# Two edge tiles ahead of the next two, and W_ih's loads later: the opening of a graph network kernel

## The chip, the cores and the metric

The kernel runs on one core of a Trainium2 chip. The metric is the device time of one execution in microseconds (us), lower is better. TensorE is called PE, VectorE DVE, ScalarE ACT, GpSimd POOL; SyncE (SP) issues most of the DMAs.

## The reference, cut to what matters

```python
h = layernorm(x)                                   # x: 10000 nodes x 512
m_in = concatenate([h[src], edge_attr], axis=1)    # 2500 edges x (512 + 128)
m = relu(m_in @ W1.T + b1) @ W2.T + b2             # edge network
agg = segment_sum(m, dst, num_segments=10000)      # sums over edges of one node
gi = agg @ W_ih.T + b_ih                           # 3 x 512 gate inputs
gh = h @ W_hh.T + b_hh
r = sigmoid(i_r + h_r); z = sigmoid(i_z + h_z); n = tanh(i_n + r * h_n)
h_new = (1 - z) * n + z * h
x = x + h + batchnorm(h_new)
x = x + mixture_of_experts(layernorm(x))           # 8 experts, the best 2, one shared
```

All arrays are float32. Matrix products are done in three passes over a high and a low part of each operand (high x high, high x low, low x high), so each operand has to be split: ACT copies out the high part, DVE subtracts it for the low part.

## The kernel before, in words

The 2500 edges are padded to 2560, 20 tiles of 128 rows, in five groups of four tiles (SUP = 4). For each group: POOL gathers the source rows of x by indirect DMA (gather_source, L697), DVE takes their statistics (stats), POOL makes the scale and shift (front), ACT normalises the rows (normalise, L806), PE transposes them four blocks a tile (transposes, L1271), ACT takes the high part of the transposed rows (transposed_hi, L817) and DVE the low part (transposed_lo, L954). The fifth block of each edge tile is the edge attributes, which arrive already transposed by DMA (attributes, L589) and are split by attributes_hi (ACT, L801) and attributes_lo (DVE, L929). layer1 (PE, L1290) then multiplies with W1, 15 matmuls of 512 columns a tile. It alternates between banks 0 and 1. DVE adds b1 (messages, L980), which empties the bank, ACT and DVE split the result (messages_hi L824, messages_lo L985), and sums (L1338) adds up rows of equal destination by a matmul with a 0/1 matrix (compare, L967) into banks 0, 1, 6 and 7. These sums are split by sums_hi (L829) and sums_lo (L998).

Once, between the second group's first layer and its sums, fused_weights multiplies W2 with W_ih (L1306 and L1321), so that the second layer and the gate product become one product. For it the four chunks of W_ih (768 KB each) are loaded, split on ACT (wih_hi_of, L801) and on DVE (wih_lo_of, L929), and W2 likewise (w2_lo, L1105). All later groups do layer1, product and sums. After the edges a loop runs over 79 tiles of nodes.

Every engine has its own queue, whose order is written out by hand; engines wait for one another on semaphores, and an instruction that waits holds all that follow on its engine. SP's queue holds the loads in the order of the program text, and a wait in it holds the loads behind it.

The waits that the prediction uses: layer1 of group 1 waits for attributes_lo(1) and, before tiles 0 and 1, for a_lo_done (the sums in banks 0 and 1 have been read); before tiles 2 and 3 it waits for msg_done (messages of tiles 0 and 1 have emptied the bank):

```python
if j < 2:
    wait_from(pe, a_lo_done, DK * (g - 1) + j + 1)
else:
    pe.wait_ge(msg_done, SUP * g + j - 1)
```

SP's attributes(1) waits for the end of layer1(0) (l1), since it overwrites the first group's attributes. A gather for tile j of group 1 waits until the same tile of group 0 is transposed (t_e). keep_running(n) issues n transposes of the identity on PE into a bank that nobody reads.

Of the kernel before, what the change touches and what calls it, by code (L numbers as in the profile page):

```python
# [34 lines left out]
def gnn_ffn(nc, x, src, dst, dst_rows, dst_back, attr_t, w1t, b1, w2, b2, wih_t, whh_t, whh, x_cols, b_ih, b_hh, gamma, beta,  # L35
# [5 lines left out]
    DK = D // P  # L41
# [7 lines left out]
    SUP = 4  # L49
# [103 lines left out]
    w2_hi = place("w2_hi", [P, DK, D], F32R)  # L153
# [429 lines left out]
    with nc.Block() as block:  # L583
        @block.sync
        def _(sp):
# [25 lines left out]
            sp.dma_start(w2_raw[:, :, :], w2v).then_inc(w2_in, 16)  # L611
            sp.dma_start(row_i[:, :], dst_rows[0:1, :].broadcast_to((R, SW))).then_inc(row_in, 16)
            sp.dma_start(b2_col[:, :], b2).then_inc(b2_in, 16)
            for k in range(2):
                sp.dma_start(wih_raw[:, k, :], wihv[:, k, :]).then_inc(wih_in[k], 16)
            sp.dma_start(ig_bias[:, :], bcast(b_ih)).then_inc(bias_in, 16)
            sp.dma_start(ig_bhh[:, :], bcast(b_hh[0:2 * D])).then_inc(bias_in, 16)
            for k in range(2, DK):
                sp.dma_start(wih_raw[:, k, :], wihv[:, k, :]).then_inc(wih_in[k], 16)
            sp.dma_start(all_dst_i[:, :], dst_back.broadcast_to((R, E))).then_inc(all_dst_in, 16)  # L620
            attributes(1)
            for n, of in enumerate((gamma, beta, run_mean, run_var)):
# [176 lines left out]
        def _(act):  # L799
# [14 lines left out]
            def transposed_hi(g, j):  # L814
                wait_from(act, l1, DK * g)
                act.wait_ge(t_e, SUP * g + j + 1)
                act.activation(m_hi[:, 0:DK, j * R:(j + 1) * R],  # L817
                               bank_of_rows(g, j)[:, 0:DK * R].rearrange("p (k r) -> p k r", k=DK),
                               ACT.Copy).then_inc(t_hi, 1)
# [24 lines left out]
                act.wait_ge(w1_in[n], 16)  # L844
                hi_of(w1_hi[:, at, :], w1_raw[:, at, :]).then_inc(w1_hi_done, 1)
            attributes_hi(0)
            for of in HALVES:
                normalise(0, of)
            for j in range(SUP):
                transposed_hi(0, j)  # L850
            act.wait_ge(w2_in, 16)
            hi_of(w2_hi[:, :, :], w2_raw[:, :, :]).then_inc(w2_hi_done, 1)
            act.wait_ge(b2_in, 16)
# [73 lines left out]
        def _(dve):  # L927
            def lo_of(lo, raw, hi):
                return dve.tensor_tensor(lo, raw, hi.bitcast(F32), ALU.subtract)  # L929
# [14 lines left out]
            def wih_lo_of(k):  # L944
                dve.wait_ge(wih_hi_done, k + 1)
                lo_of(wih_lo[:, k, :], wih_raw[:, k, :], wih_hi[:, k, :]).then_inc(wih_lo_done, 1)

            def attributes_lo(g):
                dve.wait_ge(attr_hi, g + 1)
                lo_of(m_lo[:, K1 - 1, :], m_raw[:, K1 - 1, :], m_hi[:, K1 - 1, :]).then_inc(attr_lo, 1)  # L950
# [150 lines left out]
            attributes_lo(0)  # L1101
            for j in range(SUP):
                transposed_lo(0, j)
            dve.wait_ge(w2_hi_done, 1)
            lo_of(w2_lo[:, :, :], w2_raw[:, :, :], w2_hi[:, :, :]).then_inc(w2_lo_done, 1)  # L1105
            dve.wait_ge(dst_in, 16)
            dve.wait_ge(dst_f_done, 2)
            dve.tensor_copy(dst_f[:, 0:EC], dst_i[:, :]).then_inc(dst_f_done, 1)
# [14 lines left out]
            dve.wait_ge(bias_in, 32)  # L1123
            dve.tensor_tensor(ig_bias[:, 0:2 * D], ig_bias[:, 0:2 * D], ig_bhh[:, :], ALU.add).then_inc(bias_done, 1)
            attributes_lo(1)
            wih_lo_of(0)
            for f in range(DK):
                sums_lo(0, slice(f, f + 1))
# [133 lines left out]
        def _(pe):  # L1262
            def transposes(g, j):
                pe.wait_ge(h_e, SUP * g + j + 1)

                if g == 1:
                    pe.wait_ge(t_lo, j + 1)
                elif g > 1:
                    pe.wait_ge(t_lo, SUP * g + j - 1)
                for k in range(DK):  # L1270
                    last = pe.transpose(bank_of_rows(g, j)[:, k * R:(k + 1) * R], xs[:, j, k * P:(k + 1) * P],  # L1271
                                        ident[0:R, 0:R])
                last.then_inc(t_e, 1)
# [89 lines left out]
            def keep_running(n):  # L1363

                for _ in range(n):
                    pe.transpose(bank[7][:, 0:P], ident[:, :], ident[:, :])

            pe.wait_ge(consts, 2)
            keep_running(14)
            for j in range(SUP):  # L1370
                transposes(0, j)
            keep_running(8)
            layer1(0)
            for j in range(2):
                transposes(1, j)
            sums(0)
# [415 lines left out]
```

## Time and profile before

| | us |
|---|---|
| three runs, median (lowest to highest) | 1318.66 (1316.41 to 1319.27) |
| the profiled execution, its own time | 1318.06 |
| its span in the trace | 1316.3 |

The profile is of one execution. Its times count from the start of the span; a start and a duration are given for each group of instructions, and in brackets how long the engine had been idle before it and what ended that. Matmuls overlap, so their distance from start to start, not their duration, is what PE spends on each.

### The profile page before, as it was taken

The numbers are of one execution on the slowest core, as the hardware profiler recorded it, in microseconds if no ns is written. First come the engines' busy times: TensorE is split into PE (matmuls) and PEld (weight loads), VectorE is DVE, ScalarE is ACT, GpSimd is POOL, SyncE is SP. The second block draws the span as 40 slices with busy tenths as digits, with TensorE's granted clock in tenths as the row PEclk, the third lists the DMA queues.
The fourth block names the chain that finished last, engine by engine and source line by source line (L and its number), as shares of the span: only waits on it lengthen the run. The fifth ranks groups of instructions, "written<-read, shape, count | busy, mean of one in ns | idle before, by whom it ended". The sixth has DMA issues, their size and how long they took to land. (4 is left out here: it accounts for less than half of the span.)

```text
span 1316.3 us, 22814 instructions
## 1 busy us (share of the span) xinstructions
PE 1281.1 (97%) x6360; PEld 1081.7 (82%) x6360; DVE 993.5 (75%) x2187; ACT 732.7 (56%) x1721; POOL 820.9 (62%) x1117
## 2 busy tenths in 40 slices
PE   6999999999799999999999999999999999999995
PEld 5788888888688888888888888888888888888884
DVE  6887666659587777777778778777777777877874
ACT  4420223124566666666666666666666666666652
POOL 4201152213787777777777777777777777777761
PEclk9999999999899999999999999999999999999998
DMA  8113564276333433334333333333433333433320
GB/s 328 58 33 112 176 217 169 107 282 234 139 126 127 137 120 136 126 127 135 120 128 134 121 136 126 127 136 124 133 126 127 135 120 130 133 121 137 124 97 33
DMA packets 62864, 179.58 MB, mean 136 GB/s; under 512 B 9328, under 2 KB 9968, under 8 KB 62704
## 3 DMA queue, kind: packets, MB, share of 16 engines
q1 hardware_dynamic: 46912, 99.20, 21.6%
q0 software_dynamic: 15920, 79.97, 17.7%
q8 instruction: 17, 0.28, 0.1%
q14 instruction: 15, 0.12, 0.0%
HBM read 141.86 MB, written 37.29 MB: 136 GB/s over the span
## 5 line engine op out<-in xcount | busy, mean ns | idle before, releaser
L1692 PE MATMUL bank<-whh_hi,x_hi 128*128 128x512 f32 x948 | 377.7, 398 | 7.0 <-DVE x L1638 6.6
L1692 PE MATMUL bank<-whh_hi,x_lo 128*128 128x512 f32 x948 | 370.6, 391 | 0.0
L1692 PE MATMUL bank<-whh_lo,x_hi 128*128 128x512 f32 x948 | 370.2, 391 | 0.0
L1692 PEld LDWEIGHTS bank<-whh_hi,x_hi 128*128 128x128 f32 x948 | 178.6, 188 | 43.4 <-DVE x L1638 7.0
L1692 PEld LDWEIGHTS bank<-whh_hi,x_lo 128*128 128x128 f32 x948 | 178.3, 188 | 38.4
L1692 PEld LDWEIGHTS bank<-whh_lo,x_hi 128*128 128x128 f32 x948 | 178.8, 189 | 34.6
L1511 POOL TENSOR_TENSOR h_n<-h,n_gate 128x512 f32<-128x512 f32 x79 | 102.6, 1299 | 67.1 <-ACT n_gate L1562 67.1
L1453 POOL TENSOR_TENSOR rstd<-var_eps,minus_half 128x1 f32<-128x1 f32 x158 | 90.4, 572 | 64.6 <-DVE var_eps L492 64.5
L1600 DVE TENSOR_TENSOR h_lo<-bank,h_hi 128x512 fp32r<-128x512 f32 x79 | 54.7, 692 | 82.0 <-ACT h_hi L1553 82.0
L1444 POOL DMA_INDIRECT gates<-gates_in,slot_at x79 | 85.3, 1080 | 47.6 <-issue 47.6
L1505 POOL TENSOR_TENSOR n_pre<-r_hn,gates 128x512 f32<-128x512 f32 x79 | 101.9, 1289 | 13.4 <-POOL r_hn L1501 13.2
L1501 POOL TENSOR_TENSOR r_hn<-r_gate,hn 128x512 f32<-128x512 f32 x79 | 101.2, 1281 | 2.9 <-DVE hn L1586 1.3
L534 POOL TENSOR_TENSOR x_lo<-x_lo_raw,x_hi 128x512 fp32r<-128x512 f32 x77 | 100.9, 1310 | 2.5
L1729 PE MATMUL bank<-f_hi,h_hi 128*128 128x296 f32 x316 | 101.3, 321 | 0.8 <-DVE h_lo L1600 0.8
L1493 POOL TENSOR_TENSOR x_h_b<-x_h,bn_shift 128x512 f32<-128x512 f32 x78 | 101.0, 1295 | 0.0
L1729 PE MATMUL bank<-f_lo,h_hi 128*128 128x296 f32 x316 | 95.1, 301 | 0.0
L1729 PE MATMUL bank<-f_hi,h_lo 128*128 128x296 f32 x316 | 94.5, 299 | 0.0
L1358 PE MATMUL bank<-wih_hi,a_hi 128*128 128x512 f32 x240 | 93.9, 391 | 0.0
L1358 PE MATMUL bank<-wih_lo,a_hi 128*128 128x512 f32 x240 | 93.4, 389 | 0.0
L1358 PE MATMUL bank<-wih_hi,a_lo 128*128 128x512 f32 x240 | 93.4, 389 | 0.0
L715 POOL DMA_INDIRECT g_out<-gates_in,carry_at x16 | 16.4, 1027 | 122.4 <-DMA gates_in<-g_out 99.2
L1553 ACT ACTIVATE h_hi<-bank 128x512 fp32r<-128x512 f32 x79 | 47.3, 599 | 77.8 <-PE bank L539 77.8
(196 smaller groups left out, 3089.1 us busy)
## 6 DMA issues: line engine op xcount, KB each, us to landing
xt<-in_x SPq DMA_DIRECT2D x79, 256.0 KB, 2.8
x_lo_raw<-in_x_cols SPq DMA_DIRECT2D x79, 256.0 KB, 2.6
out<-y SPq DMA_DIRECT2D x79, 256.0 KB, 2.0
gates_in<-g_out SPq DMA_DIRECT2D x16, 768.0 KB, 3.9
wih_lo_raw<-in_wih_t SPq DMA_DIRECT2D x4, 768.0 KB, 12.4
whh_rows<-in_whh SPq DMA_DIRECT2D x4, 768.0 KB, 5.8
whh_lo_raw<-in_whh_t SPq DMA_DIRECT2D x4, 768.0 KB, 9.8
gates_in<-g_out SPq DMA_DIRECT2D x12, 256.0 KB, 4.2
```

Source lines behind the costliest of these rows:

```text
L534: eng.tensor_tensor(x_lo[:, s, :], x_raw[:, s, :], x_hi[:, s, :].bitcast(F32), ALU.subtract)\
L1358: last = pe.matmul(to[0:R, :], a[:, k, j * R:(j + 1) * R], w[:, k, q * D:(q + 1) * D], start=n == 0, stop=n == 3 * DK - 1)
L1444: pool.indirect_dma_start(out=gates[:, s, :], out_offset=None, in_=gates_in, in_offset=bass.IndirectOffsetOnAxis(ap=slot_at[:, s:s + 1], a ...
L1453: pool.tensor_tensor(rstd[which][:, of:of + 1], var_eps[which][:, :], minus_half[0:R, 0:1], ALU.pow)\
L1493: pool.tensor_tensor(x_h_b[:, s, :], x_h[:, s, :], bn_shift[:, :], ALU.add).then_inc(x_h_b_done, 1)
L1501: pool.tensor_tensor(r_hn[:, :], r_gate[:, :], hn[:, s, :], ALU.mult).then_inc(r_hn_done, 1)
L1505: pool.tensor_tensor(n_pre[:, :], r_hn[:, :], gates[:, s, 2 * D:G3], ALU.add).then_inc(n_pre_done, 1)
L1511: pool.tensor_tensor(h_n[:, :], h[:, s, :], n_gate[:, s, :], ALU.subtract).then_inc(h_n_done, 1)
L1553: act.activation(h2_hi[:, :], b_th2[:, 0:DK * R], ACT.Copy).then_inc(h2_hi_done, 1)
L1600: dve.tensor_tensor(h2_lo[:, :], b_th2[:, 0:DK * R], h2_hi[:, :].bitcast(F32), ALU.subtract)\
L1692: last = pe.matmul(to[0:R, :], a[:, s, k * R:(k + 1) * R], w[:, k, q * D:(q + 1) * D], start=n == 0, stop=n == 3 * DK - 1)
L1729: last = pe.matmul(b_f1[0:R, 0:F1], a[:, k * R:(k + 1) * R], w[:, k, 0:F1], start=n == 0, stop=n == 3 * DK - 1)
```

## The change

On SP all four loads of W_ih, and with them everything behind, wait until the first gather of group 1 has landed (xs_in[0] at 32), and the loads of b_ih and b_hh follow them. On ACT the high parts of tiles 0 and 1 are taken before tiles 2 and 3 are normalised. On DVE the low part of W2 moves from behind the first group's transposed rows to behind the second group's attributes. On PE the first layer of tile 0 comes ahead of the transposes of tiles 2 and 3, and there are 6 warm-up transposes in place of 8.

```diff
@@ SP
             sp.dma_start(b2_col[:, :], b2).then_inc(b2_in, 16)
-            for k in range(2):
+
+            sp.wait_ge(xs_in[0], 32)
+            for k in range(DK):
                 sp.dma_start(wih_raw[:, k, :], wihv[:, k, :]).then_inc(wih_in[k], 16)
             sp.dma_start(ig_bias[:, :], bcast(b_ih)).then_inc(bias_in, 16)
             sp.dma_start(ig_bhh[:, :], bcast(b_hh[0:2 * D])).then_inc(bias_in, 16)
-            for k in range(2, DK):
-                sp.dma_start(wih_raw[:, k, :], wihv[:, k, :]).then_inc(wih_in[k], 16)
             sp.dma_start(all_dst_i[:, :], dst_back.broadcast_to((R, E))).then_inc(all_dst_in, 16)
             attributes(1)
@@ ACT
-            for of in HALVES:
+            for n, of in enumerate(HALVES):
                 normalise(0, of)
-            for j in range(SUP):
-                transposed_hi(0, j)
+                for j in (2 * n, 2 * n + 1):
+                    transposed_hi(0, j)
             act.wait_ge(w2_in, 16)
@@ DVE
             for j in range(SUP):
                 transposed_lo(0, j)
-            dve.wait_ge(w2_hi_done, 1)
-            lo_of(w2_lo[:, :, :], w2_raw[:, :, :], w2_hi[:, :, :]).then_inc(w2_lo_done, 1)
             dve.wait_ge(dst_in, 16)
@@ DVE
             attributes_lo(1)
+            dve.wait_ge(w2_hi_done, 1)
+            lo_of(w2_lo[:, :, :], w2_raw[:, :, :], w2_hi[:, :, :]).then_inc(w2_lo_done, 1)
             wih_lo_of(0)
@@ PE
             keep_running(14)
-            for j in range(SUP):
+            for j in range(2):
                 transposes(0, j)
-            keep_running(8)
-            layer1(0)
+            keep_running(6)
+            layer1(0, (0,))
+            for j in range(2, SUP):
+                transposes(0, j)
+            layer1(0, range(1, SUP))
             for j in range(2):
                 transposes(1, j)
             sums(0)
```

## Rows read from the trace of the kernel before

**Rows 1.** The page: busy time of PE, share of the span, instructions.

```profile
PE 1281.1 (97%) x6360; PEld 1081.7 (82%) x6360; DVE 993.5 (75%) x2187; ACT 732.7 (56%) x1721; POOL 820.9 (62%) x1117
```

**Rows 2.** What PE waited for, whole run: us in total, times, longest.

```profile
PE bank L1692 <- DVE x L1638: 6.6, 1, 6.6
...
PE bank L1338 <- DVE msg_lo L985: 1.3, 1, 1.3
```

**Rows 3.** PE in order of time: start us, us, operation, count.

```profile
13.09 1.36 PE L1271 MATMUL bank<-ident,xs 128*128 128x128 f32 x8 [0.48 <-ACT xs L806]
...
17.73 0.48 PE L1290 MATMUL bank<-w_hi,m_hi 128*128 128x512 f32 x1
...
34.26 0.47 PE L1338 MATMUL bank<-same,msg_hi 128*128 128x512 f32 x1 [1.29 <-DVE msg_lo L985]
...
41.64 1.04 PE L1271 MATMUL bank<-ident,xs 128*128 128x128 f32 x8
42.44 0.47 PE L1290 MATMUL bank<-w_hi,m_hi 128*128 128x512 f32 x1
...
49.34 0.39 PE L1290 MATMUL bank<-w_hi,m_hi 128*128 128x512 f32 x1
...
56.13 0.39 PE L1306 MATMUL bank<-wih_hi,b_hi 128*128 128x512 f32 x1
```

**Rows 4.** ACT in order of time.

```profile
16.30 2.04 ACT L817 ACTIVATE m_hi<-bank 128x512 fp32r<-128x512 f32 x4
...
35.63 0.63 ACT L801 ACTIVATE m_hi<-m_lo_raw 128x512 fp32r<-128x512 f32 x1
```

**Rows 5.** DVE in order of time.

```profile
16.90 2.48 DVE L954 TENSOR_TENSOR m_lo<-bank,m_hi 128x512 fp32r<-128x512 f32 x4 [2.30 <-ACT m_hi L817]
20.17 2.29 DVE L929 TENSOR_TENSOR w_lo<-w_lo_raw,w_hi 128x2048 fp32r<-128x2048 f32 x1 [0.78 <-ACT w_hi L801]
...
37.67 1.76 DVE L929 TENSOR_TENSOR wih_lo<-wih_lo_raw,wih_hi 128x1536 fp32r<-128x1536 f32 x1 [0.62 <-ACT wih_hi L801]
39.35 0.68 DVE L998 TENSOR_TENSOR a_lo<-bank,a_hi 128x512 fp32r<-128x512 f32 x1
...
47.94 0.68 DVE L980 TENSOR_TENSOR msg_lo_raw<-bank,b_row 128x512 f32<-128x512 f32 x1
```

**Rows 6.** POOL's gather, then SP's issues, in order of time.

```profile
15.74 1.06 POOL L697 DMA_INDIRECT xs<-in_x,src_i  x1 [0.17 <-issue]
...
12.68 0.70 SPq L615 DMA_DIRECT2D wih_lo_raw<-in_wih_t  x1
...
31.62 0.33 SPq L589 DMA_DIRECT2D m_lo_raw<-in_attr_t  x1
```

**Rows 7.** Landings (issued 1.2, 12.7, 15.7, 15.9, 31.6, 45.1): KB, us from issue.

```profile
w_lo_raw<-in_w1t SPq DMA_DIRECT2D x1, 768.0 KB, 4.7
...
wih_lo_raw<-in_wih_t SPq DMA_DIRECT2D x1, 768.0 KB, 7.9
...
xs<-in_x,src_i POOLq DMA_INDIRECT x1, 7.1
...
all_dst_i<-in_dst_back SPq DMA_DIRECT2D x1, 1280.0 KB, 19.0
...
m_lo_raw<-in_attr_t SPq DMA_DIRECT2D x1, 256.0 KB, 3.9
...
xs<-in_x,src_i POOLq DMA_INDIRECT x1, 3.6
```

**Rows 8.** SP's DMA queue at 31-32 and 33-34 us: packets, MB, share.

```profile
q1 hardware_dynamic: 46, 0.43, 100.3%
...
q1 hardware_dynamic: 169, 0.30, 81.4%
```

**Rows 9.** Windows behind PE's 6.6 us wait; the number after POOL is PE's clock.

```profile
340.00:345.00 5.00, 2.20 (x5) 1.81 (x6) 4.67 (x10) 3.45 (x8) 3.73 (x8) 0.60 0.35 114
345.00:350.00 5.00, 4.83 (x22) 3.74 (x22) 1.88 (x3) 2.72 (x5) 3.99 (x5) 0.72 0.11 43
```

## The prediction

> **What bounds the kernel now.** I read the page first: TensorE (PE) is busy for 1281.1 of the 1316.3 us span [rows 1]. Then the list of what PE waited for over the whole run [rows 2]: 1.3 us ahead of the first sums, 6.6 us where the last edge group gives way to the loop over nodes, and besides the time before its first instruction and the drain at the end little else. So between 17.73 us, where the first layer starts, and the end of the edge part the PE queue is nearly solid, and the other engines' busy shares say little about the end. An edit counts by how far it moves PE's place in its own queue, and the place to measure that is the first matmul after the second group's first layer, L1306 at 56.13 [rows 3]. What follows it up to the node loop is solid PE work, and the waits later on are for work that PE itself released, so a shift there should reach the end unchanged. The change must then be read in two stretches: 13 to 18 us, where it works on purpose, and 31 to 56 us, where its moved DMAs and its moved VectorE (DVE) step arrive.
>
> **The start.** The four transposes of tile 0 start at 13.09 and, with tile 1's, are issued by about 14.4 [rows 3]; tile 0's end near 13.84. ScalarE (ACT) takes its first high part only at 16.30, behind the normalising of tiles 2 and 3, and DVE its first low part at 16.90 [rows 4, 5]. New order: ACT has just finished normalising tile 1 then, so the high part of tile 0 starts at about 13.9 and ends at 14.45 (four took 2.04 us). DVE was idle for 2.3 us before 16.90, so attributes_lo leaves it free at 14.6; then 0.62 us for tile 0's low part. A first-layer matmul followed the low part by 0.15 us (sums: 34.26 after a low part that ended at 34.11; here 17.73 after 16.90 + 0.62). So the first layer starts at 15.33 and not 17.73: 2.4 us won. Against it, the eight transposes of tiles 2 and 3 now stand between tile 0 and tile 1: 42.44 - 41.64 = 0.8 us for eight [rows 3]. The warm-up transposes, 8 before and 6 now, cost nothing in either order, as they end when the low part does. Tile 1's low part is ready by 15.9, tile 2's by 20.5 (PE reaches that tile at 22.9), so nothing else waits. The 60 matmuls of layer1(0) take 13.8 us (30 of them 49.34 - 42.44 = 6.9), so it ended at 31.5 and now does at 31.5 - 2.4 + 0.8 = 29.9, a gain of 1.6 us. DVE without w2_lo (2.2 us at 20.17 [rows 5]) has messages(0, 0) done by 22.0, which tile 2 needs at 22.9.
>
> **To the first sums.** DVE then is 1.2 us earlier at stats(1), near 24.8: it had stood 2.3 us at 16.90 and 0.8 us at 20.17 [rows 5], now waits 4.1 us for tile 2's high part, and has 2.2 us less to do. The later chain (stats, GpSimd's power, ACT's normalising, ACT's high parts, DVE's low parts) keeps its length, so sums(0) start at about 33.0 against 34.26, and after 41.64 - 34.26 = 7.38 us of sums and 0.8 us of transposes PE asks for the second group's first layer at 41.1, against 42.44: 1.3 us early. GpSimd's gathers of tiles 2 and 3 of group 1 now wait for those tiles' transposes, and the last is issued at about 20.6; if it took 7.1 us as another did [rows 7], it would land at 27.7 and hold stats(1), which wants it at 26.6, by 1.1 us. The next stall covers that.
>
> **The DMA stream.** SP issues W_ih at 12.68 now, directly behind W2's loads, and its first chunk lands 7.9 us later, at 20.6 [rows 6, 7]. The new wait holds SP until the first gather of group 1 has landed. That gather is issued at 15.74 by GpSimd [rows 6] and took 7.1 us, in competition with W_ih [rows 7]. Without it the bounds are the quickest gather, 3.6 us (19.3), and 7.1 us (22.8); I take 3.9 us, near the quick one, as only the tail of W2 and row_i is in the way: 19.6. A chunk of 768 KB on a free queue took 4.7 us from issue (W1's first) [rows 7], so W_ih's first chunk lands at 24.3 to 24.4, 3.8 us later than before. Behind the SP wait stand the four W_ih chunks, b_ih, b_hh, all_dst, the second group's attributes, four small rows, the node table and row_i; 5.8 MB up to all_dst (5,632 KB), at 0.43 MB per us, whatever their order [rows 8]. Two of four gathers (0.52 MB, 1.2 us) no longer lie inside that stretch, so its end moves by 3.8 - 1.2 = 2.6 us. Who waits at the end of it? attributes(1) is issued at 31.62 and lands 3.9 us later, at 35.5; all_dst lands at 15.88 + 19.0 = 34.9 [rows 6, 7]. In the DMA rows the 46 packets from 31 to 32 us carry 0.43 MB, 9 KB each, which are all_dst's rows of 10 KB; the 169 from 33 to 34 carry 0.30 MB, the small ones of the attributes among them [rows 8]: the attributes move behind all_dst. I take them to land at 35.5 + 2.6 = 38.1 (call it A), although they are now issued at 30.0.
>
> The Trainium skill, "DMA: Bandwidth & Descriptors", section on queues, rings and completion order, says that each DMA engine consumes the descriptors of one ring in order; the packet sizes agree. By that rule A is 38.1. Were it not so, A would be 30.0 + 3.9 = 33.9 and the sum would be the first rival's.
>
> **What a late A costs.** On ACT attributes_hi(1) starts at 35.63 now, as soon as ACT is free and the data there, and ahead of wih_hi(0) and sums_hi(0) [rows 4]. In the new kernel ACT reaches it at 34.4 and waits to 38.1, with everything behind it. On DVE attributes_lo(1) follows that high part, 0.67 us after its start (its 0.63 [rows 4] and 0.04 to pass on); so A + 0.1 + 0.67. Then 0.6 for itself, 2.2 for the moved w2_lo, 1.68 for wih_lo(0) (39.35 - 37.67), and the first a_lo starts at A + 5.3 [rows 5]. Tile 0 of layer1(1) writes the bank that a_lo(0) reads, so PE starts it at A + 5.3 + 0.68 + 0.15 = A + 6.1 = 44.2, and stands idle for 3.1 us from 41.1. From a_lo(0) DVE is solid to messages(1, 0): 47.94 - 39.35 = 8.59 us of low parts of W_ih, sums and rows [rows 5]. Tile 2 of layer1(1) takes the bank that messages(1, 0) reads: it can start at A + 5.26 + 8.59 + 0.68 + 0.15 = A + 14.7 = 52.8. Before, PE started it at 49.34 with DVE 0.7 us ahead (47.94 + 0.68 = 48.62) [rows 3, 5]. Tile 3 needs messages(1, 1), with count(0) between; both keep their distance to messages(1, 0), which left tile 3 without a wait before, so it is not held. So L1306 comes 52.8 - 49.34 = 3.4 us later than 56.13. The 1.6 us won at the start is lost in these stalls, since both the DMA chain and the DVE chain, not PE, set this place; w2_lo was covered before by DVE's wait for the first products, and now lies on the chain. It breaks even at A = 34.7.
>
> **Rest.** stats(2), GpSimd's bn steps, SP's bn_rows, attributes(2) and the search over all_dst all hang on messages(1, 3) and move with it; all_dst, landing near 37.5, is read only behind attributes_lo(2), a whole stage later. b_ih and b_hh, due on DVE at 34.0, land at about 34 (the first chunk at 24.3, then 4.2 MB with the gathers); even 2 us late they vanish under A. ACT has slack: its wih_hi(k) come one a_hi ahead of DVE.
>
> **Sum.** -2.4 + 0.8 at the start, undone; +3.4 us at the end. Against the profiled execution (1318.06, which is its span and 1.8) that gives 1321.5; the median of the runs is 1318.66, 0.6 higher, so 1322.0. What a measurement of this kernel can tell from no change is about 0.2%, 2.6 us. Bounds for the gather's landing (3.6 and 7.1 us) put the shift at +3.1 and +6.6; if a free chunk lands after 3.9 us (as the smaller attributes did) and not 4.7, the low end is +2.3. The likeliest case's own range is +2.3 to +4.9, 1321 to 1323.6, as 7.1 was measured under the very traffic that is removed.
>
> **Rivals.** *First, not slower:* the attributes land early, A at or below 34.4. It needs either packets of attributes(1) to pass all_dst, or W_ih's stream to end no later than before. Then DVE runs from ig_bias's add (to 35.2) through attributes_lo, w2_lo and the same chain, messages(1, 0) ends at 49.0 and PE takes tile 2 at 49.1: -0.2 us; were DVE's chain 1 us shorter too, PE's own -1.3. For it speaks that its issue comes 1.6 us earlier; against it the packet sizes. It decides below A = 34.7. Chance 0.17, time 1318 (1317.3 to 1318.7). *Second:* the clock. PE's 6.6 us stall was followed by a granted clock of 0.60 and 0.72 over two stretches of 5 us, (0.8 + 0.56) x 5 = 6.8 us at 1.2 GHz where the rest is at 2.4 [rows 9]; the 1.3 us wait was not. My stalls are 3.1 and 1.7 us, between the two. A fall at 44 us would take 3.4 us of work from tiles 0 and 1, of which 1.7 is hidden by the wait for messages(1, 0): +5.1 us in all, 1323.8. Chance 0.12. *Third:* the stall at tile 2 is there but A is only 1 to 2 us late (shift +0.5 to +2): 1320; chance 0.13. The Trainium skill, "TensorE: Matmul & The Clock Gate", section "HAM oscillation", says that PE waiting on a DMA between bursts of matmuls goes back to the low clock and starts the next burst there; the second rival is what that rule would make of the 3.1 us stall. The rows agree for 6.6 us and for 1.3 us, the first with a fall, the second without one, and show nothing between. Forecast as worked out: 0.58.
>
> **How the numbers follow.** Slower by over 0.2% is A above 37.3: most of the forecast (0.47 of 0.58) and the clock case (0.12), 0.59. Within 0.2%: the rest of the forecast (0.11), the third rival (0.13) and 0.10 of the first, 0.34. Faster by over 0.2% is the first rival with more than its own arithmetic gives (a start quicker than worked out, or the fall of the clock at 341 us not happening): 0.07. The range goes from the first rival's time to half a us beyond the clock case, 1318.3 to 1324.3; about one in ten lies below and one in ten above.
>
> **What would show it.** Right: first L1290 near 15.3; W_ih issued at about 19.6; ACT's m_hi of attributes(1) near 38.2 with a wait of over 3 us for the DMA; PE idle ahead of layer1(1) until about 44 and again ahead of its tile 2; L1306 near 59.5. Wrong: ACT starts that high part before 35, or L1306 comes before 56.

## The result and the profile after

The changed kernel took 1322.87 us (median of 6 runs, 1321.46 to 1324.44), the kernel before 1318.86 beside it (6 runs, 1316.41 to 1319.82): a ratio of 1.0032, 95% interval 1.0022 to 1.0041. Slower by about 0.3%, 4.0 us between the medians. The profiled executions differ by 3.4 us: 1321.46 (span 1319.7) against 1318.06 (1316.3). The prediction was 1322.0, in a range of 1318.3 to 1324.3.

The sums of the page hardly differ from [rows 1]; the waits of TensorE do from [rows 2]. The busy times of the page:

```profile
PE 1281.8 (97%) x6358; PEld 1083.5 (82%) x6358; DVE 992.9 (75%) x2187; ACT 732.6 (56%) x1721; POOL 819.1 (62%) x1117
```

What TensorE waited for over the whole run (us in total, times, longest):

```profile
PE bank L1271 <- ACT xs L806: 4.9, 2, 4.4
...
PE bank L1338 <- DVE msg_lo L985: 0.7, 1, 0.7
```

A wait of 4.4 us for ACT's normalised rows is new, and it is not one that the prediction named. TensorE in order of time, to be laid beside [rows 3]:

```profile
15.30 0.47 PE L1290 MATMUL bank<-w_hi,m_hi 128*128 128x512 f32 x1 [0.28 <-issue]
...
18.83 1.04 PE L1271 MATMUL bank<-ident,xs 128*128 128x128 f32 x8
...
34.48 1.97 PE L1271 MATMUL bank<-ident,xs 128*128 128x128 f32 x8 [4.40 <-ACT xs L806]
37.12 0.76 PE L1338 MATMUL bank<-same,msg_hi 128*128 128x512 f32 x1 [0.68 <-DVE msg_lo L985]
...
46.19 1.03 PE L1271 MATMUL bank<-ident,xs 128*128 128x128 f32 x8
46.98 0.48 PE L1290 MATMUL bank<-w_hi,m_hi 128*128 128x512 f32 x1
...
53.96 0.47 PE L1290 MATMUL bank<-w_hi,m_hi 128*128 128x512 f32 x1
...
60.86 0.39 PE L1306 MATMUL bank<-wih_hi,b_hi 128*128 128x512 f32 x1
```

The first layer starts at 15.30, 2.4 us earlier, and the eight transposes at 18.83 are in its way for 0.8 us, both as worked out. Then the second group's transposes come at 34.48 behind 4.40 us of idleness, the sums at 37.12 and not at 33.0, and from there the sums take 46.19 - 37.12 = 9.07 us where they took 7.38. L1306 starts at 60.86, 4.7 us later than before (forecast: 3.4). Why the sums were slow stands in the windows (the number after POOL's is PE's granted clock):

```profile
30.00:35.00 5.00, 0.60 (x4) 0.52 (x4) 3.10 (x10) 1.38 (x2) 1.25 (x2) 0.89 1.02 395
35.00:40.00 5.00, 4.32 (x14) 3.38 (x13) 3.62 (x5) 4.15 (x9) 2.35 (x2) 0.50 0.94 315
40.00:45.00 5.00, 5.00 (x22) 4.07 (x21) 4.94 (x4) 5.00 (x6) 0.00 (x0) 0.93 0.12 47
```

The clock fell behind the 4.40 us, to 0.50 (1.2 of 2.4 GHz), and came back near 40.7; before, all three windows of these 15 us stood at 1.00, the middle one like this:

```profile
35.00:40.00 5.00, 5.00 (x23) 4.12 (x22) 4.38 (x6) 5.00 (x7) 0.00 (x0) 1.00 0.50 149
```

The Trainium skill, "TensorE: Matmul & The Clock Gate", section "HAM oscillation", says that waits on DMA between bursts of matmuls do this; the trace agrees, at 4.40 us.

What TensorE waited for is found by going up the chain: ACT waited 8.62 us for GpSimd's scale, GpSimd for DVE's statistics, and DVE for gathers. DVE in order of time:

```profile
24.84 1.28 DVE L936 BATCH_NORM_STATS2 st_e<-xs 128x6 f32<-128x512 f32 x2
27.85 0.69 DVE L936 BATCH_NORM_STATS2 st_e<-xs 128x6 f32<-128x512 f32 x1 [1.73 <-DMA xs<-in_x,src_i]
30.69 0.69 DVE L936 BATCH_NORM_STATS2 st_e<-xs 128x6 f32<-128x512 f32 x1 [2.15 <-DMA xs<-in_x,src_i]
...
40.06 0.69 DVE L929 TENSOR_TENSOR m_lo<-m_lo_raw,m_hi 128x512 fp32r<-128x512 f32 x1 [0.75 <-ACT m_hi L801]
40.67 2.28 DVE L929 TENSOR_TENSOR w_lo<-w_lo_raw,w_hi 128x2048 fp32r<-128x2048 f32 x1
...
44.54 0.68 DVE L998 TENSOR_TENSOR a_lo<-bank,a_hi 128x512 fp32r<-128x512 f32 x1
...
53.14 0.68 DVE L980 TENSOR_TENSOR msg_lo_raw<-bank,b_row 128x512 f32<-128x512 f32 x1
```

ACT in order of time:

```profile
33.62 1.52 ACT L806 ACTIVATE xs<-xs,nmr_e,rs_e 128x512 f32<-128x512 f32 x2 [8.62 <-POOL nmr_e L724]
...
39.40 0.63 ACT L801 ACTIVATE m_hi<-m_lo_raw 128x512 fp32r<-128x512 f32 x1 [0.85 <-DMA m_lo_raw<-in_attr_t]
```

GpSimd's issues of the first and of the last two gathers of the second group, in order of time:

```profile
15.66 1.06 POOL L697 DMA_INDIRECT xs<-in_x,src_i  x1 [0.17 <-issue]
...
19.70 0.94 POOL L697 DMA_INDIRECT xs<-in_x,src_i  x1 [1.74 <-PE bank L1271]
20.95 0.95 POOL L697 DMA_INDIRECT xs<-in_x,src_i  x1 [0.30 <-issue]
```

SP's issues:

```profile
19.09 2.35 SPq L617 DMA_DIRECT2D wih_lo_raw<-in_wih_t  x4
...
22.85 0.58 SPq L620 DMA_DIRECT2D all_dst_i<-in_dst_back  x1
30.12 0.33 SPq L589 DMA_DIRECT2D m_lo_raw<-in_attr_t  x1
```

The first gather, issued at 15.66, landed 3.4 us later. SP, released by the first, put out W_ih at 19.09; the gathers of tiles 2 and 3 came behind it, at 19.70 and 20.95, and the statistics of their rows could start only at 27.85 and 30.69, so they took 8.1 and 9.7 us to land. The second group's statistics ended 3.9 us later than with no wait, where the prediction has 1.1.

The second chain is the forecast one. The attributes, issued at 30.12, released ACT at 39.40 (forecast 38.2), 0.85 us after it was free, and all_dst had landed just before them (22.85 + 15.9 = 38.8). The Trainium skill, "DMA: Bandwidth & Descriptors", section on queues, rings and completion order, has each DMA engine consume the descriptors of one ring in order; the trace agrees: the attributes, issued 7.3 us behind all_dst, landed 0.5 us behind it. DVE then takes attributes_lo, w2_lo, wih_lo and the first a_lo at 44.54, and is solid to messages(1, 0) at 53.14. Tile 2 starts at 53.96, 14.66 us after A = 39.3; the prediction says A + 14.7.

So both chains reach tile 2 almost at once. TensorE's own (sums at 37.12, at the low clock) brings it there at 46.98 + 6.9 = 53.9, and DVE's at 53.96. One trace can't say what either is worth alone.

### The profile page after: what moved, and what is told of

It is laid out like the page before. It is cut to its first block and busy times, and to the rows that moved or that the text cites. A ratio compares the mean times of both kernels' runs of the same rounds, so it can differ in the third digit from the quotient of the medians.

```text
span 1319.7 us, 22810 instructions
## 1 busy us (share of the span) xinstructions
PE 1281.8 (97%) x6358; PEld 1083.5 (82%) x6358; DVE 992.9 (75%) x2187; ACT 732.6 (56%) x1721; POOL 819.1 (62%) x1117
```

## The experiments

They ran on two other chips: loads alone, new order alone, W2's low part on GpSimd and the kernel before once more on one (the kernel before: 1328.0 us), the rest on the other (1326.2 to 1327.3 us). Each ratio is against runs of before on the same chip, and its interval is given. The measure for the mechanism is the start of L1306's first matmul (L1307 or L1312 where an edit moved the lines): 56.13 for the kernel before on the first chip, 56.04 on the chip that ran it once more. The third chip has no trace of the kernel before, and the changed kernel was traced on the first chip only, at 60.86; differences of L1306 below are taken across the chips on the strength of that agreement.

| run | median, us | ratio (95% interval) | L1306 |
|---|---|---|---|
| loads as before | 1326.89 | 1.0002 (0.9993 to 1.0011) | 58.18 |
| w2_lo back | 1329.6 | 1.0016 (1.0006 to 1.0025) | 59.52 |
| loads alone | 1331.8 | 1.0034 (1.0022 to 1.0046) | 59.80 |
| new order alone | 1329.95 | 1.0016 (1.0004 to 1.0029) | 58.26 |
| all_dst behind | 1331.16 | 1.0029 (1.0015 to 1.0043) | 60.35 |
| TensorE kept busy | 1329.94 | 1.0020 (1.0011 to 1.0030) | 60.79 |
| both of these | 1329.86 | 1.0019 (1.0007 to 1.0031) | 59.86 |
| W2's low part on GpSimd | 1331.16 | 1.0019 (1.0006 to 1.0031) | 61.59 |
| loads apart | 1329.35 | 1.0014 (1.0003 to 1.0025) | 57.56 |
| W2 in the gap | 1328.84 | 1.0016 (1.0004 to 1.0028) | 57.56 |
| attributes first | 1326.71 | 1.0000 (0.9991 to 1.0009) | 56.47 |

### The parts of the change by themselves

**Loads as before.** SP's loads in the order and at the time of the kernel before, all else changed:

```diff
-            sp.wait_ge(xs_in[0], 32)
-            for k in range(DK):
+            for k in range(2):
                 sp.dma_start(wih_raw[:, k, :], wihv[:, k, :]).then_inc(wih_in[k], 16)
...
+            for k in range(2, DK):
+                sp.dma_start(wih_raw[:, k, :], wihv[:, k, :]).then_inc(wih_in[k], 16)
```

> The changed kernel with SP's loads in their old order and without their wait. Two chains are read in the changed kernel's trace, both ending at tile 2 of layer1(1). Chain G: the last gather of group 1 (landed 30.7) to stats(1), then 6.4 us to the first sums, then sums, transposes and two tiles. Chain D: the second group's attributes (landed 39.3) to DVE's attributes_lo, then 13.9 us to tile 2. Theory 'both chains': the gather is issued at 20.95 and lands about 7.8 us later, at 28.8; the attributes land near 35.5 and no longer bind, but attributes_lo waits for DVE's own queue, to 37.5; tile 2 at 51.3, L1306 at 58.1 (before 56.1, changed 60.9). Rival 'the attributes alone': L1306 at about 56. Rival 'the clock alone' (PE's 4.4 us idle time is what costs): PE idles only 2.8 us, no fall, L1306 near 57.1. Total between before and changed, about +2 us.

L1306 at 58.18, where both chains were to end (58.1). DVE in order of time:

```profile
27.41 0.69 DVE L936 BATCH_NORM_STATS2 st_e<-xs 128x6 f32<-128x512 f32 x1 [0.51 <-DMA xs<-in_x,src_i]
...
37.40 0.69 DVE L929 TENSOR_TENSOR m_lo<-m_lo_raw,m_hi 128x512 fp32r<-128x512 f32 x1 [1.36 <-ACT m_hi L801]
```

TensorE in the same run:

```profile
33.85 0.47 PE L1338 MATMUL bank<-same,msg_hi 128*128 128x512 f32 x1 [1.28 <-DVE msg_lo L985]
...
51.30 0.47 PE L1290 MATMUL bank<-w_hi,m_hi 128*128 128x512 f32 x1 [0.63 <-DVE msg_lo_raw L980]
```

So the loads account for 2.7 us (60.86 - 58.18), and what remains is 2.1 (58.18 - 56.04). The last gather still lands late, but holds the statistics for 0.51 us only, and the sums start 0.4 us ahead of the kernel before (34.21). They then take 8.97 us and not 7.34, at a clock of 0.74 between 35 and 40 us. Even so TensorE is 0.63 us ahead of DVE at tile 2: DVE's chain sets it, with the attributes landing 1.46 us after ACT was free, and w2_lo on the way.

**w2_lo back.** The low part of W2 is taken behind the first group's transposed rows again, all else changed:

```diff
                 transposed_lo(0, j)
+            dve.wait_ge(w2_hi_done, 1)
+            lo_of(w2_lo[:, :, :], w2_raw[:, :, :], w2_hi[:, :, :]).then_inc(w2_lo_done, 1)
...
             attributes_lo(1)
-            dve.wait_ge(w2_hi_done, 1)
-            lo_of(w2_lo[:, :, :], w2_raw[:, :, :], w2_hi[:, :, :]).then_inc(w2_lo_done, 1)
```

> The changed kernel with the low part of W2 back behind the first group's rows. Its 2.2 us leave chain D: tile 2 of layer1(1) by DVE at 51.8. Chain G is unchanged up to the sums (37.1); PE's idle time ahead of them shrinks, since messages(0, 0) come later and hold tile 2 of the first group, so the clock may stay up. Theory 'both chains': PE's own chain sets tile 2, at 52.2 with the clock up (L1306 near 59.0) or 53.8 with it down (L1306 60.7). Rival 'DVE alone' (chain G and the clock do not matter): L1306 2.2 us earlier than changed, 58.7, with the clock down as well.

L1306 at 59.52: 1.3 us better, between the two numbers that were expected. w2_lo can't go back for nothing, since the messages of tile 0 stand behind it and TensorE wants their bank earlier than before. TensorE in order of time, ahead of tile 2 of either first layer:

```profile
25.54 0.47 PE L1290 MATMUL bank<-w_hi,m_hi 128*128 128x512 f32 x1 [2.31 <-DVE msg_lo_raw L980]
...
52.61 0.47 PE L1290 MATMUL bank<-w_hi,m_hi 128*128 128x512 f32 x1 [0.90 <-DVE msg_lo_raw L980]
```

In this run attributes_lo runs at 40.14, as in the changed kernel (40.06), and tile 2 follows it by 12.5 us and not by 13.9. So w2_lo's 2.28 us on that chain are worth 1.4: without them DVE waits 0.69 us for the high part of W_ih, a wait that w2_lo had covered. Behind the 2.31 us TensorE's clock fell too (0.68 between 25 and 30 us).

**Loads alone** and **new order alone**: the kernel before with only SP's part of the change; and the kernel before with only the new order on ACT and TensorE.

```diff
# loads alone, on the kernel before
+            sp.wait_ge(xs_in[0], 32)
+            for k in range(DK):
-            for k in range(2):
                 sp.dma_start(wih_raw[:, k, :], wihv[:, k, :]).then_inc(wih_in[k], 16)
...
-            for k in range(2, DK):
-                sp.dma_start(wih_raw[:, k, :], wihv[:, k, :]).then_inc(wih_in[k], 16)
# new order alone, on the kernel before: ACT and PE as in the change, of PE only this shown
...
-            layer1(0)
+            layer1(0, (0,))
+            for j in range(2, SUP):
+                transposes(0, j)
+            layer1(0, range(1, SUP))
```

> The kernel before with the change's SP part alone: W_ih's loads wait for the first gather of group 1. The gathers are all issued by 19.6 and land near 23, so stats(1) wait for nothing and chain G stays as before. The second group's attributes land near 39, behind all_dst. Theory 'both chains': without w2_lo in it chain D is 11.7 us from attributes_lo (39.8) to tile 2 of layer1(1), 51.5; L1306 at 58.3, 2.2 us later than before. Rival 'the late gathers alone': nothing moves, 56.1.

> The kernel before with the change's order on ACT and PE alone; SP's loads and W2's low part stay where they were. The low part of W2 waits for its high part until 22.4 and then holds messages(0, 0), so PE stalls 2.3 us ahead of tile 2 of the first group (as where it was put back in the changed kernel). stats(1) start near 28.1 and find their rows, chain G gives the sums at 36.5, tile 2 of layer1(1) at 51.6, L1306 at 58.5. The attributes, issued at 34.3, land near 38.2 and chain D gives 50.7, so chain G sets it. Rival 'the early start helps as such': the order won 2.4 us at 15.3 and lost 0.8, so L1306 at 54.5.

The later loads alone cost 3.8 us at L1306, 1.5 more than expected: attributes_lo came 0.6 us later, at 40.40, and from there to tile 2 it was 12.5 us and not 11.7, by the same wait of 0.69 us for W_ih's high part. The opening was slower as well (eight transposes in 1.97 us and not 1.36, the sums 1.1 us later), but TensorE waited for DVE at tiles 0 and 2, which covers that. The gathers, three of them issued before W_ih and the last beside it (19.58 and 19.25), held nobody. ACT in that run:

```profile
39.74 0.63 ACT L801 ACTIVATE m_hi<-m_lo_raw 128x512 fp32r<-128x512 f32 x1 [2.99 <-DMA m_lo_raw<-in_attr_t]
```

And TensorE, at the sums and at tiles 0 and 2 of the second first layer:

```profile
35.33 0.47 PE L1338 MATMUL bank<-same,msg_hi 128*128 128x512 f32 x1 [1.29 <-DVE msg_lo L985]
...
44.29 0.47 PE L1290 MATMUL bank<-w_hi,m_hi 128*128 128x512 f32 x1 [0.53 <-DVE a_lo L998]
...
52.88 0.47 PE L1290 MATMUL bank<-w_hi,m_hi 128*128 128x512 f32 x1 [1.55 <-DVE msg_lo_raw L980]
```

This is the prediction's mechanism by itself, though without w2_lo: ACT 2.99 us idle for the attributes, TensorE idle ahead of tiles 0 and 2 of layer1(1). The new order alone cost 2.2 us (58.26, expected 58.5). It wins 2.4 us at the start, gives 0.8 to the transposes, and loses the rest and more in layer1(0): a 2.30 us wait for the messages behind w2_lo, and a clock that fell behind that wait (0.66 from 25 to 30 us), worth another 1.6 us. The gathers held nobody (statistics at 28.02 with no wait), and ACT waited for the last messages, so the sums came at 36.43 by TensorE's own lateness. TensorE in order of time:

```profile
25.47 0.47 PE L1290 MATMUL bank<-w_hi,m_hi 128*128 128x512 f32 x1 [2.30 <-DVE msg_lo_raw L980]
```

Neither of these two parts helps alone, and both intervals lie above 1. The move of w2_lo alone, and with the loads alone, was not run.

### Which of the two chains sets the end

**all_dst behind** issues all_dst after the second group's attributes; **TensorE kept busy** puts 40 more transposes of the identity behind layer1(0), so that TensorE does not fall idle; the third run has both edits. Nothing of the computation is left out in them.

```diff
# all_dst behind
-            sp.dma_start(all_dst_i[:, :], dst_back.broadcast_to((R, E))).then_inc(all_dst_in, 16)
             attributes(1)
+            sp.dma_start(all_dst_i[:, :], dst_back.broadcast_to((R, E))).then_inc(all_dst_in, 16)
# TensorE kept busy
             layer1(0, range(1, SUP))
+            keep_running(40)
```

> The changed kernel with the 1.3 MB load of all_dst moved behind the second group's attributes on SP. The attributes land about 3 us earlier, at 36.3. Theory 'both chains': chain G, with the clock down, still gives tile 2 at 53.8, so L1306 moves by only 0.1 to 0.3 us, to about 60.7, and the total by nothing that can be measured. The prediction's step (the attributes' landing decides one to one down to 34.7) says 3 us earlier, 57.9.

> The changed kernel with 40 more transposes of the identity on PE between the first group's first layer and the second group's transposes, about 4 us of work in a stall of 4.4 us. If they keep the granted clock up, the sums take 7.4 us and not 9.1. Theory 'both chains': chain D still holds tile 2 at about 54.0, so L1306 stays at 60.9 within 0.2. Rival 'the clock alone': 1.7 us earlier, 59.2. If transposes do not keep the clock up, the trace shows the fall as before and nothing moves.

> The changed kernel with both a3's and a4's edits: all_dst behind the second group's attributes, and 40 more transposes on PE in its stall. With the attributes early alone L1306 came at 60.35, with PE kept busy alone at 60.79. Theory 'both chains, and the half clock is part of PE's': with both gone DVE's chain starts at 38.0 and gives tile 2 at 51.9, PE's own, with sums of 7.4 us from about 35.9, gives 51.0; L1306 at 58.8, 1.5 to 2 us ahead of either alone. Rival 'the late gathers set it by themselves and neither of these matters': L1306 stays above 60.

With all_dst behind, attributes_lo ran at 37.96 with no wait for a DMA, 2.1 us earlier, and L1306 came only 0.5 us earlier (60.35). By the prediction's step, one to one from A, it should have been 58.8 (57.9 with the 3 us that were expected of the attributes). The gathers and the clock stood in its place: no wait ahead of tiles 0 and 2, and sums that took 10.0 us. TensorE in order of time:

```profile
33.22 1.36 PE L1271 MATMUL bank<-ident,xs 128*128 128x128 f32 x8 [2.90 <-ACT xs L806]
35.86 0.76 PE L1338 MATMUL bank<-same,msg_hi 128*128 128x512 f32 x1 [1.28 <-DVE msg_lo L985]
```

The window of 35 to 40 us:

```profile
35.00:40.00 5.00, 4.14 (x10) 3.29 (x11) 5.00 (x7) 4.53 (x7) 1.23 (x2) 0.50 0.92 345
```

With TensorE kept busy the clock stood at 1.00 in every window from 25 to 50 us, and the last gather held DVE's statistics for 1.6 us less than in the changed kernel (29.11 against 30.69), so the sums ended 3.3 us earlier. L1306 stayed at 60.79: the two waits that the prediction foresaw appeared at their places, because TensorE was now early enough to meet them. TensorE in order of time:

```profile
45.28 0.47 PE L1290 MATMUL bank<-w_hi,m_hi 128*128 128x512 f32 x1 [1.34 <-DVE a_lo L998]
...
53.87 0.47 PE L1290 MATMUL bank<-w_hi,m_hi 128*128 128x512 f32 x1 [1.54 <-DVE msg_lo_raw L980]
```

The same window:

```profile
35.00:40.00 5.00, 5.00 (x26) 4.04 (x24) 2.87 (x5) 3.19 (x6) 1.98 (x2) 1.00 0.94 331
```

So each chain covers the other. With both edits, and the clock at 1.00, L1306 came at 59.86, a us better than the changed kernel although the last gather landed 1.1 us later than in the run with all_dst alone (statistics at 30.50 against 29.42). Expected was 58.8. The rest is again DVE's: attributes_lo at 39.06 with no wait, and tile 2 at 52.95 behind 0.79 us for the messages, 13.9 us later, with w2_lo in between. The late gathers have a hand in that start too, since ACT takes the attributes' high part (38.27, no wait) only behind the normalised rows, which wait for them. The step from 60.8 to 59.9 is small beside the 1.5 to 2 us that were expected, and one trace each.

### Towards a better order

The runs so far name four things: gathers behind W_ih, attributes behind all_dst, w2_lo on DVE's chain, and the clock. The next runs keep the new start and move these.

**W2's low part on GpSimd.** Two W_ih chunks at once, the others behind the last gather; all_dst behind the attributes; w2_lo as an operation of GpSimd behind its gathers. **Loads apart** is the same with w2_lo where the change has it, on DVE.

```diff
-            sp.wait_ge(xs_in[0], 32)
-            for k in range(DK):
+            for k in range(2):
                 sp.dma_start(wih_raw[:, k, :], wihv[:, k, :]).then_inc(wih_in[k], 16)
+            sp.wait_ge(xs_in[SUP - 1], 32)
             sp.dma_start(ig_bias[:, :], bcast(b_ih)).then_inc(bias_in, 16)
             sp.dma_start(ig_bhh[:, :], bcast(b_hh[0:2 * D])).then_inc(bias_in, 16)
+            for k in range(2, DK):
+                sp.dma_start(wih_raw[:, k, :], wihv[:, k, :]).then_inc(wih_in[k], 16)
+            attributes(1)
             sp.dma_start(all_dst_i[:, :], dst_back.broadcast_to((R, E))).then_inc(all_dst_in, 16)
-            attributes(1)
# GpSimd, in the first of the two runs only, and w2_lo's lines taken out of DVE
+            pool.wait_ge(w2_hi_done, 1)
+            pool.tensor_tensor(w2_lo[:, :, :], w2_raw[:, :, :], w2_hi[:, :, :].bitcast(F32), ALU.subtract)\
+                .then_inc(w2_lo_done, 1)
```

> The changed kernel's order on ACT and PE, with what the two chains ask for: two chunks of W_ih are loaded at once and the rest only when all four gathers of group 1 have landed; all_dst goes behind the second group's attributes; the low part of W2 is taken by GpSimd in its 10 us of idle time, not by DVE. Theory 'both chains': the gathers land by 25, stats(1) run through from 24.8, the sums start at 33.0; attributes_lo at 36.1 or earlier gives 47.8 by chain D, PE's own chain 48.1; L1306 at 54.9, 1.3 us ahead of before, and the total 0.1% below before. Rival 'GpSimd slows DVE or its own front(1)': L1306 at 56 or later.

> The changed kernel with its loads only set right: two chunks of W_ih at once, the rest when all four gathers of group 1 have landed (25.0), all_dst behind the second group's attributes; W2's low part stays on DVE where the change put it. Both late landings are gone, and what is left is the 2.2 us of W2's low part on DVE's chain: attributes_lo at 35.4, tile 2 of layer1(1) at 49.3, L1306 at 56.1, as before, the 1.6 us of the early start used up by it. Rival 'the moved low part costs nothing once the loads are right': PE's own chain, L1306 at 55.0.

The first has the latest L1306 of all, 61.59. GpSimd in order of time:

```profile
22.70 4.60 POOL L762 TENSOR_TENSOR w_lo<-w_lo_raw,w_hi 128x2048 fp32r<-128x2048 f32 x1 [0.55 <-issue]
```

DVE in the same microseconds:

```profile
22.32 6.06 DVE L970 TENSOR_SCALAR same<-row_i,dst_f 128x512 fp32r<-128x512 int32 x4
```

Four compares that took 1.67 us in the changed kernel took 6.06 beside 4.60 us of GpSimd, so DVE was held for 4.4 us, the messages came late, TensorE waited 2.18 us at 29.13, then 2.24 and 0.83 us ahead of the sums, and the clock fell once more (0.53 between 35 and 40 us). The second, without it, had the gathers in time (statistics at 25.05 with no wait) and the sums at 33.28, where the prediction put them. L1306 at 57.56 (expected 56.1): ACT waited 1.40 us for the attributes, at 36.10, and w2_lo followed on DVE.

**W2 in the gap.** In addition W2 is split in four pieces on ACT and DVE between the transposed rows of tiles 0 and 1 and those of tiles 2 and 3, where DVE had stood idle for 4.30 us. **Attributes first**: of W_ih only the third chunk then goes ahead of the second group's attributes, the fourth and all_dst go behind them.

```diff
# W2 in the gap: ACT, DVE
                 normalise(0, of)
+                if n == 1:
+                    act.wait_ge(w2_in, 16)
+                    for k in range(DK):
+                        hi_of(w2_hi[:, k, :], w2_raw[:, k, :]).then_inc(w2_hi_done, 1)
...
-            for j in range(SUP):
+            for j in range(2):
+                transposed_lo(0, j)
+            for k in range(DK):
+                dve.wait_ge(w2_hi_done, k + 1)
+                lo_of(w2_lo[:, k, :], w2_raw[:, k, :], w2_hi[:, k, :]).then_inc(w2_lo_done, 1)
+            for j in range(2, SUP):
                 transposed_lo(0, j)
...
# attributes first: SP, in addition
-            for k in range(2, DK):
-                sp.dma_start(wih_raw[:, k, :], wihv[:, k, :]).then_inc(wih_in[k], 16)
+            sp.dma_start(wih_raw[:, 2, :], wihv[:, 2, :]).then_inc(wih_in[2], 16)
             attributes(1)
+            sp.dma_start(wih_raw[:, 3, :], wihv[:, 3, :]).then_inc(wih_in[3], 16)
```

> As d3, and W2 is split into its parts in four pieces in the gap that the new order opens: ACT between normalising tiles 2 and 3 and their high parts (idle from 16.4 to 19.5), DVE between the low parts of tiles 1 and 2 (idle from 15.8 to 20.1). Nothing of W2 is then on either chain. stats(1) at 25.0, sums at 33.2, tile 2 of layer1(1) at 48.2 by PE's own chain and 47.9 to 48.5 by DVE's; L1306 at 55.1, 1 us ahead of before; the total 0.1% below before, at the edge of what can be measured. Rival: W2's landing (17.1) or the pieces' overheads push tile 2's low part back by over 1 us, L1306 at 56.

> The changed kernel with everything that the runs so far point to: two W_ih chunks at once, the other loads behind the last gather, W2 split in four pieces in the gap of ACT and DVE, and now of W_ih only the third chunk ahead of the second group's attributes, the fourth and all_dst behind them. My theory, that in the run before this one the landing of the attributes (ACT 2.77 us idle for it) was all that held tile 2 of the second group's first layer: the attributes are issued at about 30.3 with little ahead of them, land by 34.7 when ACT is free, and ACT and DVE come 2.8 us earlier; DVE would then let PE have tile 2 at 50.64 - 2.77 = 47.9, PE itself asks for it at 33.3 + 7.38 + 0.8 + 6.9 = 48.4, so PE is solid from the sums on and L1306 starts at 55.2, 0.8 us before the kernel before (56.04). In the whole run that is 0.06%, which the times can't tell from nothing. Rival, that the attributes' own small packets need their 3.9 us or more behind whatever is in the queues, or that the fourth chunk of W_ih, now issued at about 31, is late on ACT (which wants it at 42): ACT waits for one or the other, and L1306 starts at 56.0 or later.

With W2 in the gap L1306 did not move (57.56, expected 55.1): DVE had 2.2 us less to do, of which 0.69 came back as its wait for W_ih's high part, and the attributes, 1.4 us later in this run, took the rest. ACT in order of time:

```profile
37.50 0.63 ACT L802 ACTIVATE m_hi<-m_lo_raw 128x512 fp32r<-128x512 f32 x1 [2.77 <-DMA m_lo_raw<-in_attr_t]
```

With the attributes first that wait is gone. ACT in order of time:

```profile
34.34 0.62 ACT L802 ACTIVATE m_hi<-m_lo_raw 128x512 fp32r<-128x512 f32 x1
```

TensorE waits for nothing from the sums on; they, the transposes behind them and L1306 in order of time:

```profile
33.02 0.52 PE L1344 MATMUL bank<-same,msg_hi 128*128 128x512 f32 x1 [1.28 <-DVE msg_lo L988]
...
41.98 1.03 PE L1277 MATMUL bank<-ident,xs 128*128 128x128 f32 x8
...
56.47 0.39 PE L1312 MATMUL bank<-wih_hi,b_hi 128*128 128x512 f32 x1
```

The windows from 30 to 40 us:

```profile
30.00:35.00 5.00, 3.34 (x14) 2.46 (x14) 4.12 (x6) 5.00 (x10) 2.07 (x2) 0.83 1.01 406
35.00:40.00 5.00, 5.00 (x20) 4.01 (x19) 4.44 (x5) 4.75 (x5) 0.00 (x0) 0.83 0.94 343
```

L1306 came at 56.47 and not at 55.2, because the sums took 41.98 - 33.02 = 8.96 us and not 7.38: the clock fell again, this time behind waits of 0.33 and 1.28 us. At the full clock it would have been 54.9 by an estimate (56.47 less the 1.6 us that the sums took longer), 1.1 before the kernel before; no run shows it. The whole run takes the time of the kernel before (1.0000, 0.9991 to 1.0009). Of the versions with the early start it has the earliest L1306, and its ratio lies below the changed kernel's, but it doesn't beat the kernel before.

**The kernel before, once more**, for its trace on one of the two other chips:

> The kernel before itself, for its trace on the chip that runs the others. On the first chip L1306 came at 56.1 and the first matmul of the node loop 266.2 us later. If the chip of the first four experiments is used again, the theory is that L1306 stays at 56.1 within 0.3 and that the 6 to 9 us of that chip lie between L1306 and the node loop. The rival is that the opening itself differs between chips, so that the places read there cannot be set beside 56.1.

At L1306 it is within 0.1 us of the first chip (56.04). The 7 us by which this chip is slower lie behind it, 4.7 of them in two waits of later groups' first layers, 2.8 near 190 us and 1.9 near 246, which the first chip does not have. TensorE's waits from 56 to 340 us:

```profile
PE bank L1290 <- issue: 2.8, 1, 2.8
PE bank L1290 <- DVE a_lo L998: 1.9, 1, 1.9
```

The variants, on both chips, wait at these places as well, for 4.8 to 7.6 us in all. From L1306 to the first matmul of the node loop it is 266.2 us in both kernels on the first chip, 273.2 here, and 272.7 to 277.2 in the variants. So the medians follow L1306 only roughly: 2 us more at L1306 came out as 0.05 us between the medians on one chip (loads as before, 1326.84 before) and as 2.0 on the other (new order alone, 1327.97 before).

## Why the prediction was right, and where it was not

**The start: right.** 15.30 against 15.33, the eight transposes 0.8 us, the attributes_lo and low parts of tiles 0 and 1 in time.

**The gathers: the term that was mis-sized.** The prediction gives the last gather the 7.1 us of another and a hold of 1.1 us, which "the next stall covers". It landed after 9.7 us and held the statistics by 3.9, so the sums started at 37.1 and not at 33.0. The row of 7.1 us was of a gather that W_ih met on the way; these two were issued behind W_ih. The prediction's own numbers already imply it, for the last gather at least: W_ih at 19.6 and that gather at 20.6 (measured 19.1, and 19.7 and 20.95 for the two gathers). The runs in which only two chunks leave early and the other loads wait for the last gather show the other side: statistics without a wait, sums at 33.3.

**The DMA stream and A: right in kind, 1.2 us short.** ACT's wait is for the attributes, which land behind all_dst. A was 39.3 and not 38.1, although W_ih left 0.5 us earlier than worked out. Its first chunk took 5.9 us where the prediction has the 4.7 of a free queue, so it landed at 25.0 and not at 24.3: 0.7 of the 1.2 us. Where the other 0.5 arose is not shown. That the order in the queue does it is shown by the run with all_dst behind, where DVE doesn't wait for them.

**What a late A costs: right in the distance, wrong in being alone.** Tile 2 starts at A + 14.66 (A + 14.7 worked out). But the 3.1 us of idleness ahead of tile 0 did not appear (it asked for its bank at 46.98 and had it), since TensorE was as late by the gathers. The prediction's one to one from A to L1306 failed in the run with all_dst behind (attributes_lo 2.1 us earlier, L1306 0.5); with TensorE kept busy the two predicted waits were there, at 45.28 and 53.87.

**w2_lo: right.** It lay on the chain from A, where the prediction put it. Taking it off gave 1.3 us at L1306, less than its 2.28, since DVE then waits for W_ih's high part; putting it back at its old place costs 2.3 us of TensorE's at tile 2 of layer1(0).

**The clock: the rival came true, at another place.** It was to come of a stall of 3.1 us at 44; it came of one of 4.40, ahead of the sums. It took 1.7 us from the sums, and none of it shows at the end by itself, as the run with TensorE kept busy tells (60.79 against 60.86).

**The sum.** At L1306 the shift was 4.7 us and not 3.4: 1.2 from A. The total of the profiled runs rose by 3.4 us, and the medians by 4.0. In the profiled runs 1.2 us of the shift are gone by the last node tile: the first matmul of the node loop comes 4.73 us later (327.02 against 322.29), its last 3.5 us (1291.0 against 1287.5). No wait in the lists accounts for that, and it stays open. So the 1322.0 is nearer to the measured 1322.9 than its terms deserve: that the profiled runs differ by just the 3.4 us of the forecast is luck, a late A and a loss of shift behind it that cancel. It is luck too that the gathers, whose hold of 3.9 us was put at 1.1, did not move the end: TensorE's own chain, with the slow sums, would have had tile 2 at 53.9, just ahead of DVE's 53.96.

**Not settled:** which share of the waits near 190 and 246 us belongs to the other chips and which to the variant.

## What to carry to other kernels

A transfer that is put off with a wait is not only later itself: look up which transfers are issued within a few us of its new time, since on a loaded DMA system those that come just behind it (here two gathers, 9.7 us and not 3.6) wait for it, and a wait should then name the last of them, not the first. Moving one engine's opening by 2.4 us was worth nothing here while two other chains (a transfer and an engine that does low parts) arrive at the same place; remove each alone and the other still stands, so test them in pairs. When work is moved off an idle spot of one engine, price it on the chain that it lands on.

## What the runs showed of the hardware

**Gathers.** A gather of 128 rows of 2 KB landed 3.4 to 3.6 us after its issue with little ahead of it and 8.1 and 9.7 us after it behind four chunks of 768 KB in the changed kernel. In the three runs with the same loads just ahead of both gathers (all_dst behind, TensorE kept busy, both) DVE could start on their rows 7.5 to 7.7 and 7.9 to 9.3 us after the issue, so the figure for the last one varies by 1.8 us from run to run.

**GpSimd beside DVE.** Beside a GpSimd tensor operation of 4.60 us four compares of DVE took 6.06 us and not 1.67, in one trace. The Trainium skill, "Advanced Engine Details and Errata", section "VectorE Performance Modes", says that GpSimd's instructions and those of VectorE that use two ports can block each other, because they share the second port. The trace agrees with such a block, and puts it at nearly the whole of GpSimd's operation (4.4 us); that the compares used two ports is not shown.

**The clock.** It fell behind waits of 4.40 us (the changed kernel), of 2.90 and 1.28 us (all_dst behind), of 2.31 and 2.30 us (w2_lo back 0.68, new order alone 0.66, from 25 to 30 us) and of 0.94 and 1.28 us (loads as before, 0.74 from 35 to 40 us). Behind 2.18 us at 29.13 it did not fall (W2's low part on GpSimd, 1.00 from 25 to 35). In attributes first it fell behind 0.33 and 1.28 us (0.83 over ten us), but not behind the same 0.33 and 1.28 in loads apart (1.00 in both windows). So in this kernel the length of the wait alone doesn't tell, and what does stays open. 40 transposes of the identity held it at 1.00 where it had fallen to 0.50.
